# Perceiver block on one core: first weights and tokens in smaller transfers, later ones in another order

## The reference

```python
q = heads(layernorm(x), Wq, bq, Sq)
k = heads(ctx, Wk, bk, Sk)
v = heads(ctx, Wv, bv, Sk)
q_prime = relu(einsum('bhnd,fd->bhnf', q, Wqf))
k_prime = relu(einsum('bhnd,fd->bhnf', k, Wkf)) * mask
kv = einsum('bhnf,bhne->bhfe', k_prime, v)
out = einsum('bhmf,bhfe->bhme', q_prime, kv) / (q_prime . sum(k_prime) + 1e-8)
x = x + out @ Wo.T + bo
```

## Time and profile before

| | us |
|---|---|
| median of 3 runs | 855.77 |
| lowest, highest | 855.35, 855.78 |
| the profiled execution | 855.42 |
| its span, first to last instruction | 853.6 |

### The profile page before, as it was taken

The page is one execution under the profiler, slowest core; times in us unless marked ns, Lnnn a source line. Parts: engine busy times, 40 slices in busy tenths (PEclk is TensorE's granted clock), DMA queues, the critical chain, the costliest instruction groups (busy, mean ns, idle before and its releaser), DMA issues.

```text
span 853.6 us, 14403 instructions
## 1 busy us (share of the span) xinstructions
PE 847.2 (99%) x4608; PEld 730.2 (86%) x4608; DVE 679.7 (80%) x1059; ACT 563.8 (66%) x1025; POOL 376.3 (44%) x221
## 2 busy tenths in 40 slices
PE   9999999999999999999999999999999999999998
PEld 7888888888888888888888888888888889878887
DVE  5877777777777777777777777888888878879997
ACT  6666666666666666666666666666777756677695
POOL 2655554445455554454455544454555533220210
DMA  7312123010101010010101010010101000489850
GB/s 274 99 50 97 53 75 146 27 47 25 49 25 49 25 47 26 25 49 25 49 25 49 25 42 31 25 49 25 49 25 50 26 1 1 178 315 410 320 185 13
DMA packets 19530, 66.26 MB, mean 78 GB/s; under 512 B 2224, under 2 KB 2992, under 8 KB 19120
## 3 DMA queue, kind: packets, MB, share of 16 engines
q1 hardware_dynamic: 19072, 64.88, 21.5%
q10 hardware_dynamic: 432, 1.05, 0.3%
HBM read 65.66 MB, written 0.26 MB: 77 GB/s over the span
## 4 chain that ended last, share of the span: by engine, by line
PE 98%; DVE 1%; DMA 0%; ACT 0%; issue 0%; DVEq 0%; ACTq 0%
PE side_ps L816 21%; PE side_ps L817 21%; PE side_ps L818 20%; PE kv_ps L929 11%; PE side_ps L916 11%; PE kv_ps L1213 4%; PE side_ps L1026 2%; PE side_ps L1032 2%; PE side_ps L1036 1%; PE side_ps L824 1%; PE kv_ps L824 1%; PE side_ps L1007 1%; PE kv_ps L1075 1%; DMA early<-in_wk 0%; PE kv_ps L1032 0%; PE kv_ps L1036 0%
## 5 line engine op out<-in xcount | busy, mean ns | idle before, releaser
L463 POOL TENSOR_TENSOR ksum_acc<-ksum_acc,kf 128x1024 f32<-128x1024 f32 x97 | 233.1, 2403 | 85.2 <-DVE kf L1316 85.2
L456 POOL TENSOR_TENSOR ctx_lo<-ctx_raw,ctx_hi 128x512 fp32r<-128x512 f32 x92 | 120.5, 1310 | 273.3 <-ACT ctx_hi L553 273.3
L561 ACT ACTIVATE keys<-side_ps,bias_cols 64x512 fp32r<-64x512 f32 (+1 forms) x196 | 132.5, 676 | 148.0 <-PE side_ps L818 143.0
L1292 DVE SCALAR_TENSOR_TENSOR keys<-side_ps,bias_cols,keys 64x512 fp32r<-64x512 f32 (+1 forms) x196 | 144.8, 739 | 83.8 <-ACT keys L561 80.5
L1309 DVE TENSOR_TENSOR kf<-side_ps,fb 128x256 f32<-128x256 f32 x392 | 148.7, 420 | 15.6 <-ACT fb L578 4.3
L816 PE MATMUL side_ps<-wv_hi,ctx_lo 128*128 128x512 f32 x392 | 153.9, 393 | 0.0
L817 PE MATMUL side_ps<-wv_lo,ctx_hi 128*128 128x512 f32 x392 | 153.7, 392 | 0.0
L818 PE MATMUL side_ps<-wv_hi,ctx_hi 128*128 128x512 f32 x392 | 152.5, 389 | 0.0
L816 PE MATMUL side_ps<-ctx_hi,wk_lo 128*128 128x512 f32 (+1 forms) x384 | 148.9, 388 | 0.0
L817 PE MATMUL side_ps<-ctx_lo,wk_hi 128*128 128x512 f32 (+1 forms) x384 | 148.8, 388 | 0.0
L818 PE MATMUL side_ps<-ctx_hi,wk_hi 128*128 128x512 f32 (+1 forms) x384 | 147.7, 385 | 0.0
(11 more groups left out here) (209 smaller groups left out, 967.7 us busy)
## 6 DMA issues: line engine op xcount, KB each, us to landing
ctx_raw<-in_ctx SPq DMA_DIRECT2D x46, 512.0 KB, 3.3
early<-in_stream SPq DMA_DIRECT2D x15, 1024.0 KB, 8.1
raw<-in_stream SPq DMA_DIRECT2D x12, 1024.0 KB, 9.3
early<-in_stream SPq DMA_DIRECT2D x8, 512.0 KB, 4.6
early<-in_ctx SPq DMA_DIRECT2D x2, 512.0 KB, 6.9
early<-in_wv SPq DMA_DIRECT2D x1, 1024.0 KB, 7.6
early<-in_wq SPq DMA_DIRECT2D x1, 1024.0 KB, 9.1
early<-in_wo SPq DMA_DIRECT2D x1, 1024.0 KB, 5.2
```

Source lines behind the costliest of these rows:

```text
L456: pool.tensor_tensor(ctx_lo[:, s, :, cols], raw[:, :, t % 2 * P:(t % 2 + 1) * P], ctx_hi[:, s, :, cols].bitcast(f32), ALU.subtract).then_i ...
L463: pool.tensor_tensor(ksum_acc[:, :].rearrange("p (j f) -> p j f", f=P), ksum_acc[:, :].rearrange("p (j f) -> p j f", f=P), kf[:, t % 2, :, ...
L561: act.activation(keys_2[rows, s, 2 * m + h, 0:n], src[rows, 0:n], ACT.Identity, bias=bias_cols[rows, KC + m:KC + m + 1]).then_inc(k_hi_rea ...
L1292: dve.scalar_tensor_tensor(out=keys_2[other, s, 2 * m + h, 0:n], in0=src[rows, 0:n], scalar=bias_cols[rows, KC + m:KC + m + 1], in1=keys_2 ...
```

## The change

The first key weights (m=0) come in two transfers of two depth steps each, m=1 stays third on ACT's queue, and m=2 and 3 are issued by SP, behind the first tokens. The first tokens come in three transfers: depth step 0, depth step 1, steps 2 and 3. On SP the latents and the second tokens are issued ahead of `bdk` and the biases. The splits follow the parts, and PE multiplies high with high of step 0 as soon as that step is there, then of step 1 (`keys_0_left`). The second product of `keep_warm` has 256 columns instead of 512. Products, sums and rounding are the same ones as before.

```diff
+        wk_loads = [(slice(0, 1), slice(0, 2)), (slice(0, 1), slice(2, 4)), (slice(1, 2), slice(0, KC)),
+                    (slice(2, 4), slice(0, KC))]
+        wk_parts = wk_loads[0:2] + [(slice(m, m + 1), slice(0, KC)) for m in range(1, KC)]
+        ctx0_parts = [(ctx_raw, slice(0, 1), 0), (ctx_raw, slice(1, 2), 0), (ctx_raw, slice(2, 4), 0),
+                      (ctx_raw_b, slice(0, 2), HALF), (ctx_raw_b, slice(2, 4), HALF)]
...
-            for b in range(2):
-                ks = ctx0_parts[b][1]
-                sp.dma_start(ctx_raw[:, ks, :], ctx_in[0, :, ks, :]).then_inc(ctxa_loaded[b], 16)
+            for i in range(3):
+                ks = ctx0_parts[i][1]
+                sp.dma_start(ctx_raw[:, ks, :], ctx_in[0, :, ks, :]).then_inc(ctxa_loaded[i], 16)
+            sp.dma_start(wk_raw[:, 2:4, :, :], wk_in[:, 2:4, :, :]).then_inc(wk_loaded[3], 16)
+            sp.dma_start(x_sb[:, :], x_in).then_inc(x_loaded, 16)
+            sp.dma_start(ctx_raw_b, ctx_in[1, :, :, :]).then_inc(ctxb_loaded, 16)
+            sp.dma_start(bdk, bdk_in).then_inc(bdk_loaded, 16)
             sp.dma_start(bias_cols[:, 0:KC], bq_in).then_inc(bias_loaded, 16)
             sp.dma_start(bias_cols[:, KC:2 * KC], bk_in).then_inc(bias_loaded, 16)
-            sp.dma_start(bdk, bdk_in).then_inc(bdk_loaded, 16)
-            sp.dma_start(x_sb[:, :], x_in).then_inc(x_loaded, 16)
-            sp.dma_start(ctx_raw_b, ctx_in[1, :, :, :]).then_inc(ctxb_loaded, 16)
...
             split_wk_high(0)
-            for i in range(2):
-                act.wait_ge(ctxa_loaded[i], 16)
-                split_ctx0_high(i)
-            for i in (1, 2, 3):
+            split_ctx0_arriving(0)
+            split_ctx0_arriving(1)
+            split_wk_high(1)
+            split_ctx0_arriving(2)
+            for i in (2, 3, 4):
                 split_wk_high(i)
...
+            def keys_0_left(m):
+
+                pe.wait_ge(wk_hi_ready, 1)
+                for k in (0, 1):
+                    pe.wait_ge(ctx0_hi_ready, k + 1)
+                    keys_0(m, 0, (k,), wk_hi, ctx_hi, start=k == 0)
+                pe.wait_ge(wk_lo_ready, 1)
+                keys_0(m, 0, (0, 1), wk_lo, ctx_hi)
+                pe.wait_ge(ctx0_lo_ready, 2)
+                keys_0(m, 0, (0, 1), wk_hi, ctx_lo)
...
-            keep_warm(2, ksum_acc[:, 0:P], ksum_acc[:, 0:D])
+            keep_warm(1, ksum_acc[:, 0:P], ksum_acc[:, 0:D])
+            pe.matmul(k_bank[:, 0:D // 2], ksum_acc[:, 0:P], ksum_acc[:, 0:D // 2], start=True, stop=True)
...
             wk_low(0)
             ctx0_low(0)
             ctx0_low(1)
-            for i in (1, 2, 3):
+            wk_low(1)
+            ctx0_low(2)
+            for i in (2, 3, 4):
                 wk_low(i)
```

More of the change, by code:

```diff
@@ L230, in perceiver_kernel @@
         ident_loaded = sem("ident_loaded")
-        wk_loaded = [sem(f"wk_loaded{i}") for i in range(3)]
-        ctxa_loaded = [sem("ctxa_loaded0"), sem("ctxa_loaded1")]
+        wk_loaded = [sem(f"wk_loaded{i}") for i in range(4)]
+        ctxa_loaded = [sem(f"ctxa_loaded{i}") for i in range(3)]
         bdk_loaded = sem("bdk_loaded")
```

45 lines of the change are left out of this document (24 added, 21 removed).

## The result

The changed kernel takes **858.95 us** (median of 6 runs, 856.13 to 860.04) against 855.56 us (855.35 to 855.78, 6 runs) of the kernel before on the same chip: a ratio of 1.0036, 95% interval 1.0026 to 1.0046. It is slower by 3.4 us, outside the range of the prediction (854.8 to 856.4), and clear of noise, though 3.4 us are only 0.4% of the time. Its runs spread over 4 us where those of before lie within 0.4, and its profiled execution is the fastest of them: 856.13 us, with a span of 854.3. The profile after therefore shows the smaller part of the loss; the rest had to be found with the experiments.

The account below looks back on a forecast made before the run. PE was taken as the bound: its wait for first operands, then about 848 us of products. m=1 at 7.27 instead of 7.60 gave -0.33 us, all else nothing: 855.4 us off the 855.77 median, range 854.8 to 856.4.

Parts of the forecast that it names:

- What bounds the kernel: Whole kernel: PE stops waiting for its first operands, then about 848 us of products; start of m=1, now 7.60, is forecast.
- the shift is carried to the end: Behind m=1: every wait is for PE's own products, so the 0.33 us gained reach the end.
- The moved transfers: Weights m=2,3 on SP, latents, second tokens, biases: all land in time, priced at nothing; thinnest cover 1.0 us.
- PE's first key product: Head of PE's work: shorter warm-up frees PE 0.85 us earlier; first key product at about 4.5 instead of 5.74.
- the chain that takes over: End of m=0: third tokens landed 5.62, split 0.63, subtracted 0.68, two products; m=1 at 7.27 against 7.60.
- The landing of the third tokens: Token queue: the third piece has the same bytes ahead as the second half had, so it lands at 5.62.
- I take nearly nothing: First transfers: 1 KB rows instead of 2 KB cost nearly nothing, as engines are not full from 3.0 to 4.0 us.
- Rival 2: First transfers: 1 KB rows cost as much as 2 KB; third tokens 0.8 to 1.5 us later, 856.3 to 857.0; 6%.
- Rival 1: PE's clock rises late, at 10.6, after shorter warm-up and gaps: net +1.56 us, 857.3; 10%, half at less than full price.
- PE still had work for 3.9 of 4.3 us: Argument against a late clock rise: from 1.76 to 6.1 PE still works about 3.9 of 4.3 us at the low level.
- the gap of 0.6 us ahead of the third tokens: PE between key products of steps 0, 1 and steps 2, 3: idle from about 5.7 to 6.3.

Follow-up runs that it names:

- e_order: Kernel before with only the new order of transfers (weights m=2,3 on SP, latents and second tokens ahead of small block and biases): 855.50 us against 855.41.
- e_fill8: Changed kernel plus eight unread products in PE's gap ahead of the third tokens, short warm-up: 857.35 us against 855.40 of the kernel before.
- e_short: Kernel before with the short warm-up alone: 856.8 us against 855.40.
- e_again: Changed kernel run once more, unedited: 858.89 us against 855.40 of the kernel before.
- e_back: Changed kernel with weights m=2,3 issued by ACT again: 858.52 us against 855.41 of the kernel before.
- e_tokonly: Kernel before with the new order of transfers and the first tokens in three transfers, whole warm-up: 857.65 us against 855.43.
- e_wkonly: Kernel before with the new order of transfers and the first weights in two transfers, whole warm-up: 856.99 us against 855.43.
- e_1krow: Kernel before with first weights and first half of tokens read in 1 KB rows, number of transfers unchanged: 856.36 us against 855.36.
- e_parts: Kernel before with first weights and first half of tokens each in two transfers of 64 partitions, 2 KB rows: 858.11 us against 855.36.
- e_warm2: Changed kernel with the whole warm-up restored: 857.64 us against 855.40 of the kernel before.
- e_early: Kernel before with the new order of transfers, warm-up started earlier and a quarter product longer: 855.49 us against 855.36.
- e_fill16: Changed kernel with the whole warm-up and sixteen unread products in the gap: 857.28 us against 855.36 of the kernel before.

## Why the prediction was wrong

**What bounds the kernel** was right. The start of m=1, and more exactly of the second half of the tokens, is what the time follows, and no product behind it became late. But "the shift is carried to the end" left out the time behind the output, which grew by 0.4 us in the changed kernel; the sum had no term for it. **The moved transfers**, priced at nothing, cost nothing (e_order). **PE's first key product** was forecast at 4.5 and came at 4.78; **the chain that takes over** was named rightly: third tokens, split, subtraction, two products. The split and the subtraction took 0.63 and 0.69 us, as taken from the earlier trace rows.

**The landing of the third tokens was mis-sized.** It "has the same bytes ahead of it as the second half had: landed at **5.62**, as now". It landed at 6.18 and 6.47 in the two profiled executions of the changed kernel, and at up to 7.6 in its variants. That step counted bytes. Where one queue alone has small rows, the counts above are nearly equal in packets and so give it about half the bytes; in the changed kernel both have them, and what made its third tokens late is not separated. "I take nearly nothing" for the small rows rested on engines that seemed to have room from 3 to 4 us. The runs don't bear that out: the rate from 2 to 5 us was 240 to 302 GB/s in the kernels with a split by depth steps and 294 to 324 in those without. Rival 2 (third tokens 0.8 to 1.5 us late, 856.3 to 857.0) named this loss and was near in size: e_fill8 takes 857.35, 0.4 of it behind the output, with third tokens that landed 1.7 us late. It had a chance of 6%. The profiled execution of after has this error and not that of the clock. It was forecast at 855.1 and took 856.13: 0.56 us are the third tokens, split at 6.20 instead of 5.64; 0.1 the two products behind the last wait, which took 0.34 us where the sum had 0.24 (m=1 at 7.95 instead of 7.27); 0.4 the time behind the output.

**The clock was the second failed step.** Rival 1 named it: a gap behind a shorter warm-up, a rise at about 10.6, 857.3 us. It had 10%. The reason given against it, that PE still had work for 3.9 of 4.3 us, was no reason: e_short has no product behind the first that waits for a transfer, loses 1.4 us and reaches the upper level at 10.3. The sum took the rise of one profile (6.1) as given and looked at the gap of 0.6 us ahead of the third tokens. The traces show that it matters whether the rise comes before the first gap: in e_again 0.37 us of idle time ahead of the first key product went with a rise at 9.3; in after the rise was there at 5.2 and the later gap of 0.96 us did no harm. The two errors feed each other: late pieces make gaps, and a gap at the slow pace went with a late rise in eight traces of nine. The Trainium skill ("TensorE: Matmul & The Clock Gate", Part 1) says that the moment of the rise differs from run to run of the same kernel; this case agrees, 5.2 in one profile of the changed kernel and 9.3 in the next. The page gives half a microsecond either way; here, with idle time ahead of the late one, it is 4 us. The prediction took the moment of one profile of before (6.1) for a property of the kernel.

**The sum, once more, from the runs.** Order of the transfers 0. Time behind the output 0.4 us. Late third tokens up to 1.5 us (e_fill8), 0.3 in the luckiest execution. Clock at least 1.5 us (changed kernel minus e_fill8), 2.5 in the one traced execution of about the typical time. Late tokens and clock overlap and are not constants: the short warm-up alone is 1.4, the token split alone 2.2, the weight split alone 1.6, and together they make 3.4, not 5.2. What I could not trace is a typical run of the changed kernel itself; e_back, with the same splits and the same warm-up, and as slow apart from the 0.4 us behind the output, stands for it. The mean granted clocks of the changed kernel's runs (1.0, 0.997, 0.998, 0.999, 0.998, 1.0) do not order its times, so they were not used.

**The range** was too narrow because both priced rivals were written as if they excluded each other. Rival 1's 857.3 and the 0.8 to 1.5 us of rival 2's late tokens together are 858.1 to 858.8, where the kernel took 858.95. That this sum comes so near is in part luck, since neither has the 0.4 us behind the output.

## What to carry to other kernels

An earlier start of TensorE is worth nothing while the piece that ends the stage comes no earlier; splitting the pieces ahead of it makes that piece later, so ask first which transfer lands last and what the split does to it. Products in a warm-up that nobody reads are not slack to be cut: removing 0.85 us of them cost 1.4 us. A gap while the clock is still low is better filled than left; one after the rise cost only its length here. Add up every execution from its first product to its end, and not only the stretch that was edited: 0.4 us of this loss lay behind the last output. Where two causes of loss feed each other, give their joint case a price and a chance of its own, and widen the range to it.

## What the runs showed of the hardware

- In the kernels in which one queue alone had rows of 1 KB, two queues in use at once moved nearly equal numbers of packets: 304 and 274 packets were 0.31 and 0.51 MB from 2 to 5 us (e_tokonly), 265 and 240 were 0.49 and 0.23 MB (e_wkonly). In two others they did not: 392 and 293 in e_1krow, 229 and 148 in e_parts, where the issues took longer.
- TensorE reached the upper level between about 5 and 14 us in executions that differ little: by 5.5 in e_order, 5.2 in after, 6.1 in before, 9.3 in e_again, 10.4 in e_short, 11.3 in e_warm2, 13.9 in e_back. Even with no gap it varied: 6.8 in e_early and 7.0 in e_fill16.
- Idle time of 0.25 to 1.94 us behind products at the slow pace went with a rise at 9.3 us or later in eight of the nine traces that have it; e_wkonly, idle for 0.53 us, was fast by 6.1. e_tokonly reached the level only at about 11, with the whole warm-up and a gap of 0.40 us at 5.95 and one of 0.17 at 7.76: key products at the slow pace in an all but unbroken row did not bring the rise any sooner.
- Once the level was up, gaps of 0.96 us (after) and 1.10 us (e_fill8) did not bring it down: the products behind them start 0.12 us apart.
- Eight unread products in the gap made the changed kernel 1.5 us faster (857.35 against 858.89). Sixteen of them on the critical path, beside the whole warm-up, cost nothing (857.28 against 857.64).
- From the landing of the last output to the end, 2.2 us passed in nine of the traced executions and 2.6 in seven, the two of the changed kernel among them. What decides it stays open.
